# Linear attention: masked dense and sparse scores go to the matrix engine one by one, and its small matmuls alternate between halves of the array

## What is computed

```python
def chunk_gla(q, k, v, gk, C=64):
    g = jnp.cumsum(gc, axis=1)                  # gc: gk cut into chunks of C rows
    qg = qc * jnp.exp(g); kg = kc * jnp.exp(-g)
    A = jnp.einsum('cthd,cshd->chts', qg, kg) * jnp.tril(jnp.ones((C, C)))
    o_intra = jnp.einsum('chts,cshe->cthe', A, vc)
    # and from chunk to chunk: o_inter = qg S;  S = S * exp(g_last) + k_out^T v
    return (o_intra + o_inter).reshape(L, h, dv)
gk1 = log_sigmoid(x @ Wg1a @ Wg1b + bg1) / 16   # gk2 alike
k2 = softmax(x @ Wka @ Wkb)                     # over the 64 of a head
e = softmax(x @ We); mask = one_hot(argmax(e), 4); rw = e * mask
o = chunk_gla(q1, k1, v, gk1) \
  + sum over the 4 experts of chunk_gla(q2 * rw, k2 * rw, v, gk2 * mask)
g = x @ Wga @ Wgb
o = o * lax.rsqrt(jnp.mean(o * o, axis=-1, keepdims=True) + 1e-5) * norm_w
o = (o * (g * sigmoid(g))).reshape(B, L, 512) @ Wo
```

## Time and profile before

| | |
|---|---|
| median of 3 runs | 5708.47 us |
| lowest and highest | 5705.07, 5719.47 us |
| profiled execution: its own time | 5707.32 us |
| profiled execution: span from first to last instruction | 5705.6 us |
| linear attention, from its first to its last squaring (L2105) | 4665.4 to 5691.2 us of the span |
| granted TensorE clock, mean over the span | 0.911 |
| busy share of the span: PE, PEld, DVE, ACT, POOL | 87, 45, 76, 55, 16% |

### The profile page before, as it was taken

The page is one execution under the profiler, slowest core; times in us unless marked ns, Lnnn a source line. Parts: engine busy times, 40 slices in busy tenths (PEclk is TensorE's granted clock), DMA queues, the critical chain, the costliest instruction groups (busy, mean ns, idle before and its releaser), DMA issues. The chain is left out here.

```text
span 5705.6 us, 106962 instructions
## 1 busy us (share of the span) xinstructions
PE 4935.7 (87%) x37182; PEld 2590.9 (45%) x37184; DVE 4319.6 (76%) x5246; ACT 3134.2 (55%) x5403; POOL 940.8 (16%) x886
## 2 busy tenths in 40 slices
PE   6589999999999999999952548558999879999998
PEld 3233333333333333333332336435666556777776
DVE  4589999999999999999646313377665557777776
ACT  1068888888888888888841212112222234444443
POOL 0000000000000000000005740254320023334333
PEclk8689999999999999999965779879999979999998
DMA  5322333323322222222102027622110121000000
GB/s 184 110 93 89 103 101 99 96 91 100 101 90 78 80 82 82 76 83 80 46 33 75 16 65 226 198 91 70 59 37 1 65 69 27 24 22 22 27 23 14
DMA packets 241630, 431.82 MB, mean 76 GB/s; under 512 B 37946, under 2 KB 142411, under 8 KB 239009
## 3 DMA queue, kind: packets, MB, share of 16 engines
q1 hardware_dynamic: 197424, 355.18, 19.9%
q0 software_dynamic: 26928, 62.99, 3.4%
q10 hardware_dynamic: 16896, 8.39, 0.6%
HBM read 329.36 MB, written 133.89 MB: 81 GB/s over the span
## 5 line engine op out<-in xcount | busy, mean ns | idle before, releaser
L579 DVE TENSOR_REDUCE attn_mpart<-attn_ps_max 128x2 f32<-128x1024 f32 x2048 | 2498.5, 1225 | 114.2 <-PE attn_ps_max L617 105.8
L524 ACT ACTIVATE attn_probs<-attn_ps_exp 128x512 f32<-128x512 f32 x4096 | 2221.6, 595 | 344.7 <-PE attn_ps_exp L633 100.8
L617 PE MATMUL attn_ps_max<-attn_keys,attn_quer 54*128 54x512 f32 x4096 | 1502.0, 461 | 80.3 <-DMA attn_keys<-k_laid 53.2
L633 PE MATMUL attn_ps_exp<-attn_quer,attn_keys 54*128 54x512 f32 x4096 | 1501.9, 449 | 20.4 <-issue 13.4
L648 PE MATMUL attn_ps_out<-attn_probs,attn_vals 128*32 128x256 f32 x16384 | 1318.3, 394 | 8.4 <-ACT attn_o_sb L530 7.8
L633 PEld LDWEIGHTS attn_ps_exp<-attn_quer,attn_keys 54*128 54x128 f32 x4096 | 615.4, 186 | 874.5 <-ACT attn_probs L524 837.6
L648 PEld LDWEIGHTS attn_ps_out<-attn_probs,attn_vals 128*32 128x32 f32 x16384 | 323.9, 108 | 751.5 <-issue 396.4
L617 PEld LDWEIGHTS attn_ps_max<-attn_keys,attn_quer 54*128 54x128 f32 x4096 | 603.2, 190 | 121.6 <-DVE attn_mpart L579 63.5
L1371 POOL DMA_INDIRECT ra_rows<-y_rows,slots x256 | 255.0, 996 | 318.2 <-DVE ra_total L1538 246.5
L1442 PE MATMUL ra_psO<-ra_vals,ra_probT 128*128 128x256 f32 x1152 | 273.4, 383 | 7.1 <-DVE ra_probT L1616 7.0
L734 POOL DMA_INDIRECT x_rows<-pay,slots x256 | 256.5, 1002 | 126.6 <-issue 126.6
(11 more groups left out here) (324 smaller groups left out, 5997.5 us busy)
## 6 DMA issues: line engine op xcount, KB each, us to landing
attn_keys<-k_laid SPq DMA_DIRECT2D x256, 304.0 KB
attn_vals<-v_aug SPq DMA_DIRECT2D x128, 512.0 KB, 15.0
attn_keys<-k_laid SPq DMA_DIRECT2D x256, 128.0 KB
x_rows<-attn_zeros POOLq DMA_DIRECT2D x16, 1280.0 KB, 9.7
exp_x<-x_rows SPq DMA_DIRECT2D x64, 320.0 KB
exp_w1w<-in_w SPq DMA_DIRECT2D x64, 256.0 KB
y_rows<-exp_y SPq DMA_DIRECT2D x64, 256.0 KB
q_laid<-proj_parts SPq DMA_DIRECT2D x32, 256.0 KB
```

The costliest lines, as they stand in the source:

```text
L524: act.activation(probs[k % 2][:, j, :], ps_exp[bank_of(g, n)][:, :], ACT.Exp).then_inc(exp_done, 1)
L579: dve.tensor_reduce(mpart[i][:, kb, TC * pair + tile::TC * NPR], ps_max[u % 2][:, :, :], AX, ALU.max).then_inc(unit_read, 1)
L617: mm = pe.matmul(ps_max[u % 2][:, h, :], quer[g][half(h), pair, tile * P:(tile + 1) * P], keys[g % 2][half(h), pair, kb * CH:(kb + 1) * CH ...
L633: pe.matmul(ps_exp[bank_of(g, n)][:, :], keys[g % 2][half(h), pair, k * P:(k + 1) * P], quer[g][half(h), pair, :], start=True, stop=True). ...
```

## The change

- `scores` is called once per kind, and within a kind it alternates even and odd heads, so that consecutive matmuls read different halves of the rows; even heads go to psW1, odd ones to psW0, as before. `decay_sums` is moved between the two kinds and computes each head by itself on half of the output columns, alternating; the number of its matmuls doubles.
- `keys_values` runs over pairs of heads and alternates the two heads of a pair within each expert; the number of matmuls stays 40.
- `intra` multiplies a1 and a2 by the values one after the other, each in two halves of 64 tokens: 32 matmuls with 64 columns of weights in place of 8 with 128. GpSimd's `add_scores` is gone, and `intra` waits for the fourth mask.
- On VectorE the scaling and the gating of the tile before come between the two kinds of masks. Dense and sparse states lie in one tile each (s_end, s_mid), with one instruction in place of two.
- The reciprocal root of the mean square goes from ScalarE (Ln, Exp) to GpSimd (`root`: add eps, raise to the power -0.5), ahead of `queries`. The mean's factor 1/64 is in ScalarE's Square.
- The norm weight is multiplied once into the output weights wo, before TensorE starts, in place of into every tile's gate; it is loaded by two small DMAs, one for each half of the partitions.
- ScalarE computes the exponential of the decays between Exp and Ln of the next tile's gates.

```diff
@@ states, PSUM
-        s1_end, s2_end = sb("s1_end", [P, NPAIR, DK]), sb("s2_end", [P, NPAIR, NE, DK])
-        s1_mid, s2_mid = sb("s1_mid", [P, NPAIR, 2, DK]), sb("s2_mid", [P, NPAIR, NE, 2, DK])
+        s_end, s_mid = sb("s_end", [P, NPAIR, NS, DK]), sb("s_mid", [P, NPAIR, NS, 2, DK])
-        psS2 = pb("psS2", [P, NPAIR, NE, DK])
-        psS1 = pb("psS1", [P, CH])
+        psS = pb("psS", [P, 3 * CH])
...
@@ gpsimd
-                def add_scores(tile):
-                    m, _, i = tile
-                    hold(pool, scores_masked, 4 * m + 4, pool_passed)
-                    pool.tensor_tensor(a1[:, :, :], a1[:, :, :], a2[:, :, :], ALU.add).then_inc(a_ready, 1)
+                def root(tile):
+                    m, _, i = tile
+                    hold(pool, ms_ready, m + 1, pool_passed)
+                    pool.tensor_tensor(ms[:, :], ms[:, :], eps[:, :], ALU.add).then_inc(eps_added, 1)
+                    hold(pool, eps_added, m + 1, pool_passed)
+                    pool.tensor_tensor(ms[:, :], ms[:, :], power[:, :], ALU.pow).then_inc(rms_ready, 1)
+
                 def iteration(nxt, cur, prv):
+                    if prv is not None:
+                        root(prv)
                     queries(cur)
                     if nxt is not None:
                         half_masks(nxt)
-                    add_scores(cur)
...
@@ scalar, iteration
                     copy_feats(cur)
                     if nxt is not None:
-                        log_sigmoids(nxt)
-                    if prv is not None:
-                        rms(prv)
-                    decays(cur)
+                        log_sigmoids(nxt, cur)
+                    else:
+                        decays(cur)
...
@@ vector
-                dve.wait_ge(w_loaded, 96)
+                dve.wait_ge(w_loaded, 112)
+                dve.tensor_scalar(wo[:, :, :], wo[:, :, :], nw[:, 0:1], None, ALU.mult).then_inc(wo_set, 1)
...
-                    dve.tensor_tensor(gs[i][:, :], zb[:, 2, :], ls[i][:, 2, :], ALU.mult).then_inc(y_step, 1)
-                    dve.wait_ge(y_step, m + 1)
-                    dve.tensor_tensor(gs[i][:, :].rearrange("p (h d) -> p h d", h=HL),
-                                      gs[i][:, :].rearrange("p (h d) -> p h d", h=HL),
-                                      nw[:, :].unsqueeze(1).to_broadcast([P, HL, DK]), ALU.mult).then_inc(gate_ready, 1)
+                    dve.tensor_tensor(gs[i][:, :], zb[:, 2, :], ls[i][:, 2, :], ALU.mult).then_inc(gate_ready, 1)
...
-                    mask_scores(cur)
+                    mask_scores(cur, 0)
                     if prv is not None:
+                        scale_o(prv)
                         gated(prv)
+                    mask_scores(cur, 1)
...
@@ tensor
-                def scores(tile):
-                    m, _, i = tile
-                    pe.wait_ge(feats_copied, 4 * m + 4)
-                    for x in range(4):
-                        if x >= 2:
-                            pe.wait_ge(scores_masked, 4 * m + x - 1)
-
-                        r = x % 2 * DK
-                        for b in range(NPAIR):
-                            mm = pe.matmul(psW[(x + 1) % 2][:, b * P:(b + 1) * P], ftT[r:r + DK, x // 2 * 2, b, :],
-                                           ftT[r:r + DK, x // 2 * 2 + 1, b, :], start=True, stop=True)
-                        mm.then_inc(scores_summed, 1)
+                def scores(tile, kind):
+
+                    m, _, i = tile
+                    if kind:
+                        pe.wait_ge(scores_masked, 4 * m + 2)
+                    else:
+                        pe.wait_ge(feats_copied, 4 * m + 4)
+                    for b in range(NPAIR):
+                        for odd in range(2):
+                            r = odd * DK
+                            mm = pe.matmul(psW[1 - odd][:, b * P:(b + 1) * P], ftT[r:r + DK, 2 * kind, b, :],
+                                           ftT[r:r + DK, 2 * kind + 1, b, :], start=True, stop=True)
+                            if b == NPAIR - 1:
+                                mm.then_inc(scores_summed, 1)
...
                     for b in range(NPAIR):
-                        pe.matmul(pdec1[:, b, :], ls[i][:, 0, b * P:(b + 1) * P], halves[:, :], start=True, stop=True)
+                        for odd in range(2):
+                            rows, head = slice(odd * DK, odd * DK + DK), slice((2 * b + odd) * DK, (2 * b + odd + 1) * DK)
+                            pe.matmul(pdec[rows, b, 0, :], ls[i][:, 0, head], halves[:, :], start=True, stop=True)
...
-                    for hh in range(HL):
-                        head, rows = slice(hh * DK, (hh + 1) * DK), slice(hh % 2 * DK, hh % 2 * DK + DK)
-                        for e in range(NE):
-                            pe.matmul(psS2[rows, hh // 2, e, :], ke[i][:, e, head], v[i][:, head], start=True, stop=True)
-                        mm = pe.matmul(kv1[rows, hh // 2, :], kg1[i][:, head], v[i][:, head], start=True, stop=True)
+                    for b in range(NPAIR):
+                        for e in range(NS):
+                            for odd in range(2):
+                                head, rows = slice((2 * b + odd) * DK, (2 * b + odd + 1) * DK), slice(odd * DK, odd * DK + DK)
+                                keys = ke[i][:, e - 1, head] if e else kg1[i][:, head]
+                                mm = pe.matmul(kv[rows, b, e, :], keys, v[i][:, head], start=True, stop=True)
...
-                    pe.wait_ge(a_ready, m + 1)
+                    pe.wait_ge(scores_masked, 4 * m + 4)
...
                     for hh in range(HL):
-                        pe.matmul(psO[:, hh, :], a1[:, hh, :], v[i][:, hh * DK:(hh + 1) * DK],
-                                  start=(hh == 0), stop=False, skip_group_check=True)
+                        for a in (a1, a2):
+                            for late in range(2):
+                                rows = slice(late * GC, late * GC + GC)
+                                pe.matmul(psO[rows, hh, :], a[:, hh, rows], v[i][:, hh * DK:(hh + 1) * DK],
+                                          start=(hh == 0 and a is a1), stop=False, skip_group_check=True)
...
                     ahead(ZG, K2)
+                    scores(cur, 0)
                     decay_sums(cur)
-                    scores(cur)
+                    scores(cur, 1)
                     ahead(Q2, V)
```

More of the change, by code:

```diff
@@ L2041, in iteration @@
                         half_masks(nxt)
-                    add_scores(cur)
                     if nxt is not None:
                         keys(nxt)
-                run(pool, prologue, iteration, lambda tile: None)
+                run(pool, prologue, iteration, root)
             @block.scalar
@@ L2165, in gated @@
                                       ALU.mult).then_inc(o_read, 1)
+                def gated(tile):
+                    m, _, i = tile
                     dve.wait_ge(o_read, m + 1)
@@ L2177, in center, with mask_scores @@
                                       ALU.subtract).then_inc(k_centered, 1)
-                def mask_scores(tile):
+                def mask_scores(tile, kind):
                     m, _, i = tile
-                    for x in range(4):
+                    for x in (2 * kind, 2 * kind + 1):
                         dve.wait_ge(scores_summed, 4 * m + x + 1)
@@ L2295, in epilogue @@
                     mean_square(tile)
+                    scale_o(tile)
                     gated(tile)
```

97 lines of the change are left out of this document (43 added, 54 removed).

## The result

| | before | after |
|---|---|---|
| median (4 runs each on the same chip) | 5711.43 us | 5544.34 us |
| lowest and highest | 5705.07, 5719.47 us | 5541.61, 5548.02 us |
| ratio, 95% interval | | 0.9707 (0.969 to 0.9724) |
| profiled execution: its own time, span | 5707.32, 5705.6 us | 5545.91, 5544.2 us |
| first to last squaring, 31 intervals | 1025.8 us | 859.9 us |

The kernel became faster by 167 us, where 95 were forecast: the sign is right, and 5544 lies in the range 5540 to 5665, though only 4 us inside its lower edge. Nearly the whole difference lies in one term.

What follows compares the result with a forecast made beforehand. PE was taken to bound the stage, VectorE second. Tile 32.3 - 1.7 - 1.7 - 1.15 = 27.75, with the clock 30.3; 30 x (33.31 - 30.35) = 89, with the ends 96, giving 5613 us, range 5540 to 5665.

Steps and rivals of the forecast that it cites:

- (b): Scores on PE with alternating row halves: 0.9 us per kind for 1.71; gain together with the decay sums 1.7 us.
- (c): Decay sums on half columns, between the kinds of scores: 0.95 us for 1.88, then a PE wait of 1.0.
- (d): PE's 1.69 us wait before the transposes of the gated output (L2353) goes with the root on GpSimd: gain 1.7.
- (e): Keys times values on PE, heads of a pair alternating: 2.4 us for 3.56, gain 1.15; bad end 4.64.
- (f): Intra on PE, 64 records: 1.9 us with overlap, 3.7 without; 2.19 us of waiting covers it, bad case costs 1.5.
- (g): GpSimd's sum of scores (L2024), already covered before intra: taking it away is worth nothing on the path.
- (h): VectorE loses the norm-weight multiplication and other work: 25.3 to some 24 us busy a tile; worth nothing, not binding.
- (i): ScalarE loses two small operations, keeps two table loads a tile; decays' exponential at t = 8.5, needed at 11.3.
- The clock: TensorE's 1.2 GHz stretches stay as frequent but uncovered: each costs 3.4 us, in the mean 2.55 a tile; tile 30.3.
- the clock stays at 2.4 GHz: Rival: no lower-clock stretches in the stage, 172 us gained, 5536 us; denser scores for it; chance 8%.
- The slower rivals: Overlap as today, 5732 us, or none, near 5775 (together 9%); GpSimd's power over 6 us or wider low clock, 3%.
- The ends: Outside the 30 intervals: last interval 4.5 us, first tile 3, end 1.2, start -1.7.

Runs made afterwards that it cites:

- Q2 in the wait: Changed kernel with Q2 projected between the decay sums and the second kind of scores: 5513.95 us against 5552.22 of the changed kernel; 0.9651 of before.

## Why the prediction was right, and where its sum was off

Put shortly: the terms of the path were right to 0.3 us a tile, and that of the clock was wrong, so that the time came out nearer to a rival's price (5536) than to the forecast (5613). That it still lies in the range, by 4 us, is partly luck.

- **(b), (c)** Right. Scores 1.06 and 1.16 where 0.9 was taken, decays 1.1 (5208.46 to about 5209.57) for 0.95, the wait 0.81 for 1.0. V starts 9.31 after Z1, for 8.95: gain 1.4, not 1.7. Undoing both costs 0.72 of it; the rest, by difference, lies in the order, with decays behind the first scores.
- **(d)** The wait of 1.69 went, by the root alone. The power took 1.64 us, where the nearest row had 0.20 and the bound was 3; it ended at 5178.91, before the first masks. In the undisturbed tile it ended 4.2 after Z1, as forecast, because GpSimd's keys were through about a microsecond sooner than forecast: two errors that cancelled. By the prediction's own list, a power of microseconds would have been a sign of being wrong; 1.64 fitted into its 3. The wait before L2353 would have been 3.2 by now, with all else faster, so the part is worth more than the 1.7 of the forecast. The gating took 0.95 in the mean, not 1.41.
- **(e)** Right: 2.48 for 2.4, and undoing it gives 1.07 of the 1.15.
- **(f), (g)** Right: intra 2.1 for 1.9 under a cover of 2.19, and the sum on GpSimd is worth nothing.
- **(h), (i)** Right: VectorE 22.78 busy for about 24, not binding.
- **Tile at full clock**: 27.97 for 27.75. The path was right to 0.2 us.
- **The clock**, the term that failed: "I see no reason for fewer or more stretches. But nothing absorbs them now: each costs 3.4, in the mean 2.55 a tile." The mean is 28.02, so it cost 0.05. Against the forecast's 30.35 this is 30 x 2.33 = 70 us of the 72 that were missing. The second sentence holds where the spot stays thin. The first failed: it set a wait of 1 us beside shorter decays and called them even, and it took the wait before the transposes for cover alone. With scores of 1.06 in place of 1.71, decays of 1.1 in place of 1.9 and no wait before the transposes, the clock stayed up in 30 of 31 intervals. It took both: with the spot thin it fell in 18 of 30 (decays and scores undone) and 14 (before, with only the root moved), and with the spot dense but the root late in 20, 21 and 25. The rival "the clock stays at 2.4 GHz" came true, with "denser scores" as half of its reason, and 8% was too little for it. Its own price, 5536, is 8 us off. The prediction's own sign, "if the clock's share leaves 0.92 by much", also said so: 1.00.
- **The slower rivals** carry two slips of sum that change nothing. By the way the forecast was added up, tiles of 34.2 and 35.6 give some 5728 and 5770 us, not 5732 and 5775, and the chances of the slower cases add up to 12%, where 0.10 stands.
- **The ends**: the last interval brought 7.3 for 4.5, the start 4.4 where first tile and preparations were to give 1.3 together, the tail 0.2 for 1.2; and 9.1 went on a later start of the stage.

What stays open is why the number of falls differs without a change ahead of the spot: 1 and 5 in two executions of one program, 12 when only keys times values is slower. The falls aren't scattered like independent draws: before has them in three tiles of every four throughout, the scores one half after the other nearly always in one of four, the decays in two of eight. So the length of a tile, which sets when the spot comes back, may matter; only Q2 in the wait gave none at all, and no run varied the length alone. That density matters stands on the early falls: 1 and 5, 8, 7, 18, of which the single steps are near this scatter and the last is not; and 23 against 9 when the kernel before gets the dense spot. The 12 with the spot dense and no long wait isn't far from the 14 and 18 with it thin, so that how much density is worth stays uncertain. That the wait matters stands on the late falls: 12, 14 and 19 in the three kernels where it is over 2 us, and none in the others, before with its 1.7 among them.

## What to carry to other kernels

Small matmuls on half of the rows or columns run at once with those on the other half if they alternate; order them so before anything else, since it costs no instruction. Then look at what the saved time turns into: at first it only became waits, until the late result of another engine (here a tiny root behind two table loads) was moved off. And count a lower clock as part of a stage that the change can end: here it took both a denser thin spot and the end of a long wait, each of which let the clock fall by itself. The stretches cost 1.00 us a tile before and would have cost 2.5 without cover; they cost 0.05. Making only the rest shorter brings stretches out of cover.

## What the runs showed of the hardware

- Between the squarings of this stage TensorE's clock falls for stretches of 3.4, 6.8 or 10.2 us. Without cover a 3.4 costs 1.65 and a 6.8 costs 3.27 us, half their length each.
- It fell behind matmuls with 2 and 8 moving columns and sparse scores though PE waited for nothing over 0.3 us (18 of 30 intervals), and, with that spot dense, in or behind a wait of 3.1 us for the output (14 of 30).
- Matmuls on different halves overlap, and start out of order. In the rows of the kernel before with the root on GpSimd, Q2's first record (L2328) starts at 5169.70, before the last three score records (L2366, 5169.81), which stand ahead of it in the program. The Trainium skill, "TensorE: Matmul & The Clock Gate", What overlaps and what doesn't, says that matmuls start in strict program order; these starts contradict it.
- Of the sixteen scores, mixed by halves of the rows, a kind takes 1.06 us where one half after the other takes 1.71; eighty records of keys times values, mixed by halves of the columns, take 2.48 where head by head takes 3.55.
- GpSimd's power with 8 values on each of 128 partitions takes 1.64 us, eight times the addition of the same shape (0.20).
- The gating on VectorE, with both sources in SBUF, took 0.69 us where no GpSimd instruction ran, in the kernel with the gate after all masks, and 0.91 to 1.05 beside GpSimd's queries in the changed one. Before, it was 1.41 in the mean, beside the sum. The rows of a disturbed tile before:
```profile
5177.96 1.74 DVE L2167 TENSOR_TENSOR gla_on<-gla_on,gla_gs 128x512 f32<-128x512 f32 x1
...
5176.80 2.35 POOL L2024 TENSOR_TENSOR gla_a<-gla_a 128x1024 f32<-128x1024 f32 x1 [2.65 <-DVE gla_a L2185]
```
The gating ends 0.55 us after the GpSimd instruction that ran when it began, here (5179.70 against 5179.15) and in the changed kernel alike: what is added depends on how much of that instruction was left. The Trainium skill, "SBUF — State Buffer", Terms, says that the port pair which VectorE and GpSimd share is held for a full instruction and that the loser is blocked meanwhile. The trace agrees.
